# Attention over sixteen groups: outputs of two key steps issued together, all column sums of a query block behind its last outputs

## The reference

```python
xn = _layernorm(x, axis=-1)                       # x: (4, 2048, 512)
q = (xn @ Wq).reshape(B, S, N_KV, GROUP, HEAD_DIM)  # N_KV = 4, GROUP = 4, HEAD_DIM = 32
k = (xn @ Wk).reshape(B, S, N_KV, HEAD_DIM)
v = (xn @ Wv).reshape(B, S, N_KV, HEAD_DIM)
scores = jnp.einsum('bqkgd,bskd->bkgqs', q, k) * scale
scores = jnp.where(causal, jnp.finfo(scores.dtype).min, scores)
attn = jax.nn.softmax(scores, axis=-1)
out = jnp.einsum('bkgqs,bskd->bqkgd', attn, v)
...
x = x + out.reshape(B, S, N_EMBD) @ Wo + ffn(xn)   # ffn: shared experts and 6 of 32 routed ones
```

## Time and profile before

| | |
|---|---|
| time, median of 3 runs | 3629.08 us (3625.17 to 3641.87) |
| the profiled execution | 3625.24 us, span 3623.5 us |
| PE busy | 3515.8 us, 97% |
| DVE, POOL, ACT busy | 2202.3, 2069.6, 1630.5 us |
| attention, 1409.8 to 3440.0 us of the span | 2030.2 us, PE busy 1981.7 us in it |

### The profile page before, as it was taken

The page is one execution under the profiler, slowest core; times in us unless marked ns, Lnnn a source line. Parts: engine busy times, 40 slices in busy tenths (PEclk is TensorE's granted clock), DMA queues, the critical chain, the costliest instruction groups (busy, mean ns, idle before and its releaser), DMA issues. The chain is left out here.

```text
span 3623.5 us, 57441 instructions
## 1 busy us (share of the span) xinstructions
PE 3515.8 (97%) x19864; PEld 2215.9 (61%) x19864; DVE 2202.3 (61%) x5314; ACT 1630.5 (45%) x3331; POOL 2069.6 (57%) x1598
## 2 busy tenths in 40 slices
PE   6999999999997999999999999999999999999999
PEld 5888888888875555555545555545555555555487
DVE  6455455555542334777777777777777777777444
ACT  3232232222221113666566666656666566666611
POOL 0333333323332223877787787778778778777800
PEclk9999999999998999999999999999999999999999
DMA  5333333333337995202202211220221222030087
GB/s 176 102 110 101 102 110 102 102 110 102 102 123 220 312 302 157 59 24 66 60 23 69 60 49 36 66 60 23 66 60 38 50 66 60 20 80 25 22 302 245
DMA packets 265836, 358.71 MB, mean 99 GB/s; under 512 B 95453, under 2 KB 105309, under 8 KB 265625
## 3 DMA queue, kind: packets, MB, share of 16 engines
q1 hardware_dynamic: 227976, 325.86, 29.9%
q0 software_dynamic: 17920, 12.82, 1.7%
q10 hardware_dynamic: 19728, 17.34, 1.4%
HBM read 234.18 MB, written 121.38 MB: 98 GB/s over the span
## 5 line engine op out<-in xcount | busy, mean ns | idle before, releaser
L1454 ACT ACTIVATE prb<-sps 128x512 f32<-128x512 f32 (+2 forms) x2521 | 1172.9, 540 | 721.2 <-PE sps L1550 692.8
L1478 DVE TENSOR_REDUCE mx<-mps 128x1 f32<-128x512 f32 x1496 | 987.8, 686 | 354.6 <-PE mps L1526 353.0
L1394 POOL TENSOR_TENSOR rows<-rows,prb 128x1024 f32<-128x1024 f32 x378 | 895.8, 2392 | 1.1 <-ACT prb L1454 1.1
L396 POOL DMA_INDIRECT tab_s<-pay,slot x384 | 376.8, 981 | 729.6 <-DVE tokf L694 489.7
L1566 PE MATMUL ops<-prb,vst 128*32 128x512 f32 (+3 forms) x5120 | 598.4, 539 | 8.9 <-ACT four L1418 7.0
L1481 DVE CUSTOM_DVE_ANT_0 mps<-mps,bias 128x512 f32<-128x512 f32 x980 | 501.7, 523 | 169.8 <-PE mps L1526 169.7
L1388 POOL TENSOR_TENSOR rows<-prb 128x1024 f32<-128x1024 f32 x192 | 455.5, 2394 | 213.8 <-ACT prb L1454 213.8
L1550 PE MATMUL sps<-w_hi,x_hi 97*128 97x512 f32 (+2 forms) x1280 | 494.5, 393 | 16.2 <-ACT prb L1454 14.1
L1550 PE MATMUL sps<-w_lo,x_lo 97*128 97x512 f32 (+1 forms) x1241 | 477.1, 393 | 19.2 <-ACT prb L1454 19.2
L1526 PE MATMUL mps<-x_lo,w_lo 96*128 96x512 f32 (+2 forms) x1280 | 474.2, 377 | 3.3 <-DVE mx L1481 2.8
L1526 PE MATMUL mps<-x_hi,w_hi 96*128 96x512 f32 (+2 forms) x1196 | 445.7, 379 | 2.9 <-DVE mx L1481 2.4
(11 more groups left out here) (173 smaller groups left out, 3887.9 us busy)
## 6 DMA issues: line engine op xcount, KB each, us to landing
wgu<-in_e_gu SPq DMA_DIRECT2D x24, 1408.0 KB, 6.4
rows<-in_x SPq DMA_DIRECT2D x16, 1024.0 KB, 7.8
xn_s<-rows SPq DMA_DIRECT2D x16, 1024.0 KB, 5.1
y_sb<-in_x SPq DMA_DIRECT2D x16, 1024.0 KB, 5.2
q_hi_s<-qk_hi SPq DMA_DIRECT2D x16, 1024.0 KB, 4.2
q_lo_s<-qk_lo SPq DMA_DIRECT2D x16, 1024.0 KB, 6.6
base<-y_sb SPq DMA_DIRECT2D x16, 1024.0 KB, 4.3
w_hi<-q_hi_s SPq DMA_DIRECT2D x64, 256.0 KB, 5.2
```

What stands on the lines that cost most here:

```text
L396: nc.gpsimd.indirect_dma_start(t["tab"], bass.IndirectOffsetOnAxis(ap=slot[:, i, k:k + 1], axis=0), pay[:, i, k, :], None, bounds_check=E ...
L1394: nc.gpsimd.tensor_tensor(acc4, acc4, prb[:, (2 * n + pr) % RP], ALU.add).then_inc(add_done, 1)
L1454: nc.scalar.activation(prb[:, (2 * k + h // 2) % RP, h % 2, q0:CH], bank(bg, GROUP * k + h)[:, q0:CH], ACT.Exp, scale=SCALE).then_inc(exp_ ...
L1478: V.tensor_reduce(mx[:, h * NKT + qt, j:j + 1], mps[:, slot, 0:wr], AX.X, ALU.max).then_inc(mred_done, 1)
```

## The change

- PE issues the scores and pieces of two steps (an even step and the next, a **pair**) without a break, and behind them the outputs of the pair before, in one burst. There are 20 bursts in a group in place of 40.
- All column sums of a block stand in one run directly behind its last outputs (`sum_of_four`, now L1675, and `sum_of_step`, L1659), in the burst of step `lasts` + 2.
- The sums have no bank of their own. Seven banks are shared: three for scores, four for pieces (three before), and a block's sums take one of these four from the run until ACT has copied it. `bank_table` writes down for each use the bank and what releases it.
- How many pieces stand behind each score comes from a list for each pair (`PIECES_OF_PAIR`).
- `prb` holds 7 steps (8 before); a third buffer for sums of four (`third_sum`); POOL's third and fourth additions next to the diagonal stand one or more steps later (`third`, `fourth`). The last sums wait on PE's side only by `sums_done`.

The core of the diff:

```diff
+PIECES_OF_PAIR = (8, 7, 8, 8, 8, 8, 9, 9, 7, 7, 11, 7, 9, 10, 8, 7, 8, 8, 8, 5)
...
-        RP = 16
+        RP, HELD = 14, 7
...
-        sps = ps("sps", [P, R, CH])
-        mps = ps("mps", [P, R, CH])
+        third_sum = sb("third_sum", [P, 2, 2, CH])
+        sums = [*psum2, [third_sum[:, q] for q in range(2)]]
+        NB = 7
+        banks = ps("banks", [P, NB, CH])
         ops = ps("ops", [P, CH])
-        dps = ps("dps", [P, CH])
...
+        def third(f, pr):
+
+            return f + 4 + pr if f + 4 in diag else f + 3
+
         def fourth(f, pr):
 
-            return f + 4 + (pr if f + 4 in diag else 0)
-
+            return f + 6 + pr if f + 4 in diag else f + 4
...
             def take_denominators(bg, j):
-                nc.scalar.activation(den[j % 2][:], dps[:], ACT.Copy).then_inc(den_done, 1)
+                act.wait_ge(sums_done, bg * JC + j + 1)
+                nc.scalar.activation(den[j % 2][:], bank("sums", bg, j), ACT.Copy).then_inc(den_done, 1)
...
-                if r >= 0 or alone:
-                    for h in range(GROUP):
-                        last = M(dps[HD * h:HD * (h + 1), q0:CH], ones[:],
-                                 prb[:, (2 * k + h // 2) % RP, h % 2, q0:CH], start=opens,
-                                 stop=(r == 3), skip_group_check=True)
-                last.then_inc(pv_done, 1)
...
+                if r == 3:
+                    for gi in fours_of(j):
+                        sum_of_four(bg, gi)
+                    for x in range(k - 3, k + 1):
+                        last = sum_of_step(bg, x)
+                    last.then_inc(sums_done, 1)
...
                     for h in range(GROUP):
                         scores(bg, p, k, h)
-                        for g, n in todo[h:h + 1]:
+                        for g, n in todo[sum(count[:h]):sum(count[:h + 1])]:
                             piece(g, n)
-                    for gi, f in enumerate(fours):
-                        if k == f + DUE:
-                            sum_of_four(bg, gi)
-                        if prev and k + NK == f + DUE:
-                            sum_of_four(bg - 1, gi)
-                    if k >= LAG:
-                        output(bg, p, k - LAG)
-                    elif prev:
-                        output(bg - 1, 1 - p, NK + k - LAG)
-                    for g, n in todo[GROUP:]:
-                        piece(g, n)
+                    if k % 2:
+                        for x in (k - 1 - LAG, k - LAG):
+                            if x >= 0:
+                                output(bg, p, x)
+                            elif prev:
+                                output(bg - 1, 1 - p, NK + x)
```

More of the change, by code:

```diff
@@ L14 @@
+from collections import deque
 from contextlib import ExitStack
@@ L869, with behind_scores @@
 AHEAD = 20
-def maxima_by_step():
-    steps, pieces = attention_steps(), maxima_pieces()
-    order = [(k + len(steps) - AHEAD) % len(steps) for k in range(len(steps))]
-    room = [0.75 if steps[k][2] >= 2 else 1.0 for k in order]
-    cost = [64 + piece[5] for piece in pieces]
-    first = []
-    for x in range(len(steps)):
-        share = sum(room[:x]) / sum(room) * sum(cost)
-        first.append(sum(1 for n in range(len(pieces)) if sum(cost[:n + 1]) <= share + 1))
-    return first + [len(pieces)]
+PIECES_OF_PAIR = (8, 7, 8, 8, 8, 8, 9, 9, 7, 7, 11, 7, 9, 10, 8, 7, 8, 8, 8, 5)
+def behind_scores(k):
+    n, u = PIECES_OF_PAIR[k // 2], 2 * GROUP
+    upto = [0] + [min(((x + 1) * n + u // 2) // u, n) for x in range(u)]
+    upto[u] = n
+    half = k % 2 * GROUP
+    return [upto[x + 1] - upto[x] for x in range(half, half + GROUP)]
+def maxima_by_step():
+    first = [0]
+    for x in range(2 * len(PIECES_OF_PAIR)):
+        first.append(first[-1] + sum(behind_scores((x - AHEAD) % (2 * len(PIECES_OF_PAIR)))))
+    assert first[-1] == len(maxima_pieces())
+    return first
 def block_ends():
@@ L1285, in maxima, with bank_table, take, outputs @@
             return [(bg, n) for n in range(first[x], first[x + 1])]
+        def bank_table():
+            scored = deque((n, "free", 0) for n in range(R))
+            reduced = deque((n, "free", 0) for n in range(R, NB))
+            held, table = [], {}
+            def take(ring, item, kind, count):
+                table[item] = ring.popleft()
+                if item[0] == "sums":
+                    bg, j = item[1:]
+                    held.append((GROUP * (NK * bg + lasts[j] + LAG + 1) + 3, (table[item][0], kind, count)))
+                else:
+                    ring.append((table[item][0], kind, count))
+            def outputs(bg, k):
+                j = steps[k][0]
+                if k == opened_at(bg, j):
+                    take(reduced if bg < END or scored else last_ring, ("sums", bg, j), "taken", bg * JC + j + 2)
+            last_ring = deque()
+            for bg in range(BG):
+                for k in range(NK):
+                    todo = maxima(bg, k)
+                    if bg == END and not todo and scored:
+                        last_ring.extend(reduced)
+                        last_ring.extend(scored)
+                        reduced.clear()
+                        scored.clear()
+                    count = behind_scores(k)
+                    for h in range(GROUP):
+                        for wait, entry in list(held):
+                            if wait <= GROUP * (NK * bg + k) + h:
+                                held.remove((wait, entry))
+                                (reduced if scored else last_ring).append(entry)
+                        take(scored or last_ring, ("score", bg, GROUP * k + h), "scored",
+                             bg * NU + GROUP * k + h + 1 + R)
+                        for g, n in todo[sum(count[:h]):sum(count[:h + 1])]:
+                            take(reduced, ("piece", g, n), "reduced", g * NM + n + 1 + R)
+                    if k % 2:
+                        for x in (k - 1 - LAG, k - LAG):
+                            if bg or x >= 0:
+                                outputs(bg + x // NK, x % NK)
+            for x in (NK - 2, NK - 1):
+                outputs(END, x)
+            return table
+        where = bank_table()
+        def bank(*item):
+            return banks[:, where[item][0], :]
         block = ctx.enter_context(nc.Block())
@@ new lines, in output, with sum_of_step @@
+                if alone:
+                    sum_of_step(bg, k).then_inc(pv_done, 1)
+                else:
+                    last.then_inc(pv_done, 1)
+                if r == 3:
[4 more added lines that the diff above has]
+                    last.then_inc(sums_done, 1)
+            def sum_of_step(bg, k):
+                j, kt, r = steps[k]
+                q0 = max(r, 0) * P
+                opens = k == (opened_at(bg, j) if fours_of(j) else lasts[j] - 3) and k != lasts[j]
+                if opens:
+                    released("sums", bg, j)
+                dps = bank("sums", bg, j)
+                for h in range(GROUP):
+                    last = M(dps[HD * h:HD * (h + 1), q0:CH], ones[:],
+                             prb[:, slot(bg, k, h // 2), h % 2, q0:CH], start=opens, stop=(r == 3),
+                             skip_group_check=True)
+                return last
@@ L1576, in sum_of_four @@
             def sum_of_four(bg, gi):
-                j, kt, _ = steps[fours[gi]]
-                opens = kt == 0 and j > 1 and not direct(bg, gi)
+                j = steps[fours[gi]][0]
+                opens = gi == fours_of(j)[0] and opened_at(bg, j) == lasts[j]
                 if opens:
-                    pe.wait_ge(den_done, bg * JC + j + 1)
+                    released("sums", bg, j)
+                dps = bank("sums", bg, j)
                 for pr in range(2):
```

96 lines of the change are left out of this document (48 added, 48 removed).

## The result

| | before | after |
|---|---|---|
| time, median of 5 runs | 3630.00 us (3625.17 to 3641.87) | 3666.93 us (3664.78 to 3674.04) |
| the profiled execution | 3625.24 us | 3674.04 us |
| attention | 2030.2 us | 2079.1 us |

The changed kernel takes 1.01 times the time of before (95% interval 1.0083 to 1.0117). The profiled executions differ by 48.8 us, and the attention alone differs by 48.9: nothing else moved. One of the ten runs of experiment 8 took 5600.45 us at a granted clock of 0.56 and is left out of its time.

What follows compares the result with a forecast made beforehand. PE's own list was taken as the bound. Terms -112 + 42 + 41 + 17 - 7 = -19, -15 with the last group, and +38 for the clock took 3625.24 to 3648, forecast 3650 us; own range 3636 to 3665, wide 3575 to 3680.

Steps and rivals of the forecast that it cites:

- The transfers inside an eight: ACT's row-maxima transfers at steps 5, 21 and 25 delay the eighth score: 46 x 1.9 = 87 us, net +41 us.
- the moved sums give nothing more: PE's sums: as many matmuls as before and already inside bursts, so no further gain from moving them.
- The clock: PE's clock falls behind 0.6 of 46 long waits: 28 falls of 1.56 us, +43 us, net +38 us.
- The burst: PE's outputs of two steps joined: 0.35 us for each of 320 bursts saved, -112 us.
- the pace of the eights: Score m + 3 waits for exponential m through a run of eight: 2.7 us a group, +42 us.
- The fourth bank: Four banks for pieces in place of three, so pieces wait less for DVE's reductions: -7 us.
- The copy of the sums: ACT's 0.48 us copy delays the sixth score about 0.4 us at 64 places: 26 us, net +17 us.
- POOL was taken as hidden: POOL's last addition of a group done about 1.2 us before PE comes to it, at no cost.
- waits for its additions at the sums: Sign that the prediction is wrong: PE waiting at the sums for POOL's additions; no size given.
- The last group: Its second half has neither pieces nor transfers, ACT bounds much of it: no change, within 4 us.
- the waits come and the clock stays: Rival, chance 0.27: PE waits at the transfers without clock falls; 3610 us, or with some falls up to 3630.
- the transfers hide: Rival, chance 0.17: eights keep their pace and held exponentials cost no more; 3530 us, or 3571 if only transfers bind.

Runs made afterwards that it cites:

- experiment 8: Experiment 1's kernel with POOL's scaling of the previous group's last block at step 12 in place of 9; 3621.73 us, ratio 0.9959 to the kernel before.
- Experiment 1: The changed kernel with the row-maxima transfers of steps 5, 21 and 25 one step later, at the next pair's start; 3553.97 us, ratio 0.9786 to the kernel before.
- experiment 7: The changed kernel with each step's outputs in a burst of their own, transfers left where the change has them; 3661.83 us, ratio 1.0077 to the kernel before.
- experiment 5: The changed kernel with two of the four transfers of steps 5, 21 and 25 one step later; 3585.62 us, ratio 0.9857 to the kernel before.
- Experiment 4: Experiment 1's kernel with each step's outputs in a burst of their own again; 3616.5 us, ratio 0.9964 to the kernel before.
- experiment 12: Experiment 1's kernel with six shared banks in place of seven; 3637.32 us, ratio 1.0017 to the kernel before.
- experiment 9: Experiment 1's kernel with ACT's copy of the sums behind the pair's eighth exponential in place of the second; 3564.11 us, ratio 0.9815 to the kernel before.
- experiment 10: The kernel of experiment 8 with SP's store of the last block behind the reciprocals in place of ahead; 3541.82 us, ratio 0.9754 to the kernel before.
- experiment 6: The kernel before, with its transfers of steps 5, 21 and 25 moved to steps 6, 22 and 26; 3676.98 us, ratio 1.0103.
- experiment 2: The changed kernel with only the transfers of step 25 moved to step 26; 3619.7 us over ten executions, ratio 0.997 to the kernel before.

## Why the prediction was right

The forecast was 3650 us, its own range 3636 to 3665 and the wide one 3575 to 3680; it came to 3666.9, slower by 1%: 2 us above its own range and inside the wide one. The mechanism that it named for the loss is the one that the experiments show; some of the sizes were off, and they partly made up for each other. Point by point:

- **The transfers inside an eight.** Predicted: eighth score 5.10 us after the first, waits of 1.5 to 2.0 us at steps 5, 21 and 25, none to speak of at 32, 33 us of waiting grown to about 80. Found: 5.12 us, waits of 1.77, 1.45 and 1.75, and 82.5 us. Experiment 1 confirms it as the cause: 113 us, where waits and falls were put at 87 and 43. Part of it comes without any eight. The prediction says that the moved sums give nothing more, but with sums and pieces moved and the bursts still single the kernel loses 28 us against before (experiment 7).
- **The clock.** Predicted: 28 falls of 1.56 us. Found: 24, one of them not behind a transfer; in the pair that was compared it cost 1.6 (12.03 against 10.43 us). The share, three of five waits of before, came near the 23 of 46 by luck: it is 14 of 15 in one place and 2 of 15 in another, and it changed from one kernel and one execution to the next. The Trainium skill's rule ("TensorE: Matmul & The Clock Gate", "Why this matters for your kernels"), which lets idle gaps be longer than these, does not hold here: in the changed kernel the clock fell behind single gaps of 1.44 to 2.41 us, in kernel 7 once behind 1.27, and in experiment 5, with gaps of 0.47, behind none of them.
- **The burst.** Predicted: 112 us won, 42 given back by the pace of the eights, 70 net. Experiment 4 measures 62.5, but its edit takes back a part of the wait for the copy of the sums as well; with that part its own expectation was 55. The joined burst took 1.85 us against 1.86 predicted.
- **The fourth bank.** Predicted: -7 us. It was not measured by itself; six banks, one fewer in all than before had, cost 83 us in eights (experiment 12). The term was too small for what depends on it.
- **The copy of the sums.** Predicted: 0.4 us at each of 64 places, net +17. It was not measured by itself. The pair of step 6 lasts 6.12 us against 5.76 at step 28, with as many pieces, and experiment 9 won back 0.2 of that; at steps 2, 14 and 26 its edit cost time, so nothing can be said of them.
- **What was mis-sized.** POOL was taken as hidden, and waits for its additions at the sums were named as a sign of being wrong. The sign came, at one place: at block 1 PE waits about 0.6 us in each of 15 groups, 8.5 us in all, and experiment 10, which takes the wait away, wins 12 us. The last group was taken as no change within 4 us and is 9 us longer; about 4 of these 9 are the wait of step 5 and a fall, which the other terms hold already. The clock, 20 falls more at 1.6, cost 32 in place of 38. With these the 3648 predicted for the profiled execution become 3648 + 12 + 5 - 6 = 3659, and it took 3674. The 15 us that are left no experiment assigns; the pace of the eights and the copy of the sums are the terms that were not measured apart.
- **The rivals.** That the waits come and the clock stays is refuted by the 24 stretches; that the transfers hide, by the 82.5 us, though experiment 1 shows that it was one step away: its price, 3530 if everything hides, lies 12 us under kernel 10 and 24 under kernel 1.

## What to carry to other kernels

Before joining two short phases into a long one, list what else stands in the partner's program inside the new long phase: the same 2.4 us of issue that cost 0.34 to 0.86 us at the end of a step cost 1.45 to 1.77 inside an eight, and nothing under a long burst. And before moving short pieces of work out of a phase, ask what they cover there: with the sums and a piece gone from in front of step 5, its wait was 1.02 us in place of 0.34 (experiment 7). Moving such work is worth trying in both directions, and each move has to be followed through the queues behind it (SP's store in experiment 8, the copies in experiment 6). A wait of PE of 1.3 us or more can cost 1.6 us more than its length here; cut to half a microsecond it won more than its length. And where such falls come and go, take several executions: one kernel, unchanged, spread over 24 us (experiment 2).

## What the runs showed of the hardware

The fall of the clock is not a property of the wait alone. Waits of 1.73 to 1.76 us, with PE busy for about half of the 3.3 or 3.4 us ahead of them, lost it in one place and kept it in the next. In the kernel that moves the transfers of step 21, the falls at step 25 were 4 where they had been 14, without a touch to the waits there, and executions of that kernel with a granted clock of 0.985 to 0.986 took some 10 us more than those with 0.988 to 0.989. In the attention of the fourteen profiles, its first scores apart, no fall stands behind a wait shorter than 1.27 us, and some waits above 2 us kept the clock (2.27 us in experiment 6). The one pair that could be compared lost 1.6 us to a stretch at half clock. And ACT's four small transfers hold its list for 2.4 us wherever they stand together, in every kernel here: that time can be placed, not saved.
